# Four accumulator banks for the first layer, and one small exponential of ScalarE in the value stage

## The chip, the cores and the metric

The kernel runs on one core of a Trainium2 chip. The metric is the device time of one execution in microseconds (us). The core has TensorE (matmuls; its results go to PSUM, which has 8 banks of 2 KB in each of 128 partitions), VectorE, ScalarE, GpSimd and SyncE, which here issues most transfers. The engines run by their own lists of instructions and meet only at semaphores.

## The reference

One layer of attention over a graph of 384 nodes with 1024 features and 16 heads of 64, with a residual and a layer norm:

```python
q = x @ wq.T + bq
k = x @ wk.T + bk
v = x @ wv.T + bv
q2 = (q @ wiq.T + biq).reshape(N, H, D).transpose(1, 0, 2)
k2 = (k @ wik.T + bik).reshape(N, H, D).transpose(1, 0, 2)
v2 = (v @ wiv.T + biv).reshape(N, H, D).transpose(1, 0, 2)
mask = _build_mask(edge_index, edge_type, edge_type_weights, x.dtype)
scores = jnp.einsum('hnd,hmd->hnm', q2, k2) * scale + mask[None]
attn = jax.nn.softmax(scores, axis=-1)
out = jnp.einsum('hnm,hmd->hnd', attn, v2)
out = out.transpose(1, 0, 2).reshape(N, OUT_F)
return out @ wo.T + bo
```

The result is `_layernorm(x + that)`. The mask (384 x 384) is filled from 6144 edges; of several edges for one cell the last one counts.

## The kernel before

**Arithmetic.** Every float32 factor is split in two: a high part in a reduced format (`w_hi`, `h_hi`), and a low part, the rest (`w_lo`, `h_lo`). A product is three matmuls: high by high, high by low, low by high (lines 888 to 890). The high part is made by ScalarE (line 393 for weights, 440 for the first layer's results), and the low part by VectorE (600, 682) or GpSimd (307) as raw minus high.

**Stages.** Weights come as 56 tiles of 128 x 1024 through a ring of RING = 4 slots. Tiles 0 to 23 are the first layer (q, k and v, eight each): each is 24 matmuls into one bank. The loop over groups (`group`, Fori from 1 to 5) handles four tiles a turn; group 0 stands ahead of it, and its tiles 0 and 1 are done together. Tiles 24 to 31 are the value stage (v2 of all nodes, in banks 0 to 5). Tiles 32 to 47 are q and k of the eight head pairs. A step of the attention handles the q and k tile of pair j on TensorE, and woven in between scores, transposes and values of pair a = j - 1. Tiles 48 to 55 are the output product, woven into the last pair.

**Order in the first layer.** For tile t TensorE waits for `w_lo` of t (`tile_ready`) and, in the loop, for `acc_free` of at least t + 1; the semaphore starts at 2, so this says that tile t - 2 has been emptied. `first_acc` (banks 4 and 5) serves tiles 0 and 1, `acc` (banks 6 and 7) all later ones by turns. A finished tile is read by ScalarE (line 440, h_hi), then by VectorE (line 682, h_lo), and this second read frees the bank. VectorE's order is: w_lo of tiles 2 to 5 with the emptying of tiles 0 to 3 between, the table of edge values (`value_table`), then eight counts of edges for group 0 (line 664, `count_later`), and then the loop. A turn of the loop is, four times over: w_lo of tile t + 2 (600), one count, emptying of tile t (682), one count. In its first turn, t is 4, so w_lo of tile 6 stands ahead of the emptying of tile 4.

**Order in the value stage and the attention.** In the value stage ScalarE makes w_hi of tile t + 2 once tile t - 2 is through (`split`). In the step of the first pair it takes the biased results of the k tile (456), two w_hi, a copy of the values (480, `v_high`), then the exponentials of five of the six score tiles (486). VectorE masks the scores (773, negated row maximum beside it), and normalises with the reciprocal of the row sums (781, 783). TensorE transposes the probs of one head once all its three tiles are normalised (977, waits `probs_ready`). VectorE's first mask waits also for `mask_loaded` and for `res_ready`, three additions of GpSimd (358) that come after its 48 scatters of mask cells (336) and three w_lo.

**Function tables of ScalarE.** Exp, Ln and Sqrt want a table loaded; the build puts a table load (ACT_TABLE_LOAD) ahead of the activation that needs another table than the one that is there. Before, there are four: at lines 388, 428 (Ln), 486 (Exp) and 568 (Sqrt). Copy and Identity run with any of these.

Of the kernel before, what the change touches and what calls it, by code (L numbers as in the profile page):

```python
# [11 lines left out]
ACT = mybir.ActivationFunctionType  # L12
ALU = mybir.AluOpType
AX_X = mybir.AxisListType.X
ds = bass.ds

P = 128
N = 384
# [20 lines left out]
RING = 4  # L39
L1_TILES = 3 * KT  # L40
IV_TILE = L1_TILES
# [9 lines left out]
FIRST_TILES = 2  # L51
# [11 lines left out]
def gnn_layer(nc, x_t, x_rows, weights, bias_cols, bias_rows, edge_weights, edge_cols, edge_rows,  # L63
              key_rows, mask_cells, out):
    with ExitStack() as ctx:
        def sb(name, shape, dt):
            return ctx.enter_context(nc.sbuf_tensor(name, shape, dt))

        def sem(name):
            return ctx.enter_context(nc.semaphore(name))  # L70
# [3 lines left out]
        x_hi, x_lo = sb("x_hi", [P, KT, N], F32R), sb("x_lo", [P, KT, N], F32R)  # L74
        att_hi, att_lo = x_hi, x_lo

        h_hi, h_lo = sb("h_hi", [P, L1_TILES, N], F32R), sb("h_lo", [P, L1_TILES, N], F32R)
# [39 lines left out]
        def x_raw(k):  # L117
# [15 lines left out]
        ew, ew_abs, ew_exp, ew_ln, ew_pos, soft = (  # L133
            sb(n, [P, ETYPES], F32) for n in ("ew", "ew_abs", "ew_exp", "ew_ln", "ew_pos", "soft"))
        zeros = sb("zeros", [P, P], F32)
# [6 lines left out]

        bank = [ctx.enter_context(nc.psum_tensor(f"bank{i}", [P, HALF], F32)) for i in range(8)]
        acc = bank[6:8]
        first_acc = bank[4:6]
        score_bank = [bank[i] for i in (0, 1, 2, 3, 0, 1)]

        def pt_bank(a, g):
# [34 lines left out]
        acc_free = sem("acc_free")  # L183
# [197 lines left out]
        def _(act):  # L381
# [8 lines left out]
            def high_part(t, s, raws):  # L390

                act.wait_ge(raw_loaded[s], 16 * raws)
                nc.scalar.activation(w_part(t, s, slice(0, F))[0], w_raw[:, s, :], ACT.Copy).then_inc(w_hi_done, 1)  # L393

            def split(t, s, raws):

                act.wait_ge(tile_done, t - RING + 1)
                high_part(t, s, raws)
# [31 lines left out]
            def group(g, first=False):  # L430
                for s in range(RING):
                    t = RING * g + s


                    if not (first and s == 0):
                        high_part(t + LEAD, (s + LEAD) % RING, g + 1 + (s + LEAD) // RING)

                    act.wait_ge(tile_done, t + 1)
                    ps = first_acc[s] if first and s < FIRST_TILES else acc[s % 2]
                    nc.scalar.activation(h_hi[:, ds(t, 1), :].rearrange("p a n -> p (a n)"), ps[:, 0:N],  # L440
                                         ACT.Identity, bias=bcol[:, ds(t, 1)]).then_inc(acc_hi, 1)

            group(0, first=True)
            with act.Fori(1, GROUPS) as g:
                group(g)


            for t in range(IV_TILE, PAIR_TILE):
                split(t + LEAD, (t + LEAD) % RING, (t + LEAD) // RING + 1)

            def evacuate(t, u, slot, which):

                act.wait_ge(tile_done, t + 1)
                for h in range(2):
                    here = slice(h * D, (h + 1) * D)
                    nc.scalar.activation((q_high, k_parts)[which][here, 2 * slot + h, :], acc[which][here, 0:N],
                                         ACT.Identity, bias=bcol[here, ds(u, 1)]).then_inc(half_hi, 1)
# [85 lines left out]
            a = PAIRS - 1  # L543
# [34 lines left out]
        def _(dve):  # L578
# [16 lines left out]
            def low_part(t, s):  # L595

                dve.wait_ge(w_hi_done, t + 1)
                cols = slice(0, F)
                hi, lo = w_part(t, s, cols)
                nc.vector.tensor_tensor(lo, w_raw[:, s, cols], hi.bitcast(F32), ALU.subtract)\  # L600
                    .then_inc(w_lo_dve, 1)
# [59 lines left out]
            def count_later(g, slot, chunks):  # L661
                for c in chunks:
                    n = P * (WC - c % WC)
                    nc.vector.scalar_tensor_tensor(  # L664
                        out=unread[:, c, 0:n],
                        in0=keyb[:, slot, P * c:P * c + n].rearrange("p a e -> p (a e)"),
                        scalar=key[:, ds(GC * g + c, 1)], in1=later[:, 0:n],
                        op0=ALU.is_equal, op1=ALU.mult, accum_out=n_later[:, ds(GC * g + c, 1)]).then_inc(dve_step, 1)
                    steps[1] += 1

            def choose_cells(g):
                mine = ds(GC * g, GC)

                dve.wait_ge(dve_step, steps[0] + steps[1])
                nc.vector.scalar_tensor_tensor(out=cell[:, mine], in0=n_later[:, mine], scalar=BEYOND,
                                               in1=key[:, mine], op0=ALU.mult, op1=ALU.add)\
                    .then_inc(cells_ready, 1)

            def evacuate(t, ps):

                dve.wait_ge(acc_hi, t + 1)
                nc.vector.scalar_tensor_tensor(  # L682
                    out=h_lo[:, ds(t, 1), :].rearrange("p a n -> p (a n)"), in0=ps[:, 0:N],
                    scalar=bcol[:, ds(t, 1)],
                    in1=h_hi[:, ds(t, 1), :].rearrange("p a n -> p (a n)").bitcast(F32),
                    op0=ALU.add, op1=ALU.subtract).then_inc(acc_free, 1)
# [3 lines left out]
            def group(g, slot):  # L690
                t = RING * g
                for s in range(RING):
                    low_part(t + LEAD + s, (LEAD + s) % RING)
                    if s == 0:

                        dve.wait_ge(rows_loaded, 16 * g + 16)
                    count_later(g, slot, range(2 * s, 2 * s + 1))
                    evacuate(t + s, acc[s % 2])
                    count_later(g, slot, range(2 * s + 1, 2 * s + 2))
                choose_cells(g)  # L700

            for t in range(FIRST_TILES):
                low_part(t + LEAD, t + LEAD)
                evacuate(t, first_acc[t])
            low_part(FIRST_TILES + LEAD, 0)
            evacuate(FIRST_TILES, acc[0])
            value_table()
            low_part(FIRST_TILES + 1 + LEAD, 1)
            evacuate(FIRST_TILES + 1, acc[1])

            dve.wait_ge(rows_loaded, 16)
            count_later(0, ds(0, 1), range(GC))
# [3 lines left out]
            with dve.Fori(1, GROUPS) as g:  # L716
                new_part(STEPS_PER_GROUP * g + (before - STEPS_PER_GROUP))
                group(g, ds(g % 2, 1))
                assert steps[1] == STEPS_PER_GROUP
# [128 lines left out]
            a = PAIRS - 1  # L848
# [7 lines left out]
            for n in range(NT):  # L856
                for i, (b, cols) in enumerate(OUT_PIECES[n]):
# [4 lines left out]
                    ins = nc.vector.bn_stats(stats[:, n, 6 * i:6 * i + 6], part)  # L862
# [14 lines left out]
        def _(pe):  # L877
            def tile_ready(t, pair_tile=False):

                if pair_tile:  # L880
                    pe.wait_ge(w_lo_pool, t + 1 - PAIR_TILE)
                else:
                    pe.wait_ge(w_lo_dve, t + 1)

            def by_outputs(out_ps, s, k, moving_hi, moving_lo):

                cols = slice(k * P, (k + 1) * P)
                pe.matmul(out_ps, w_hi[:, s, cols], moving_hi, start=(k == 0), stop=False)  # L888
                pe.matmul(out_ps, w_hi[:, s, cols], moving_lo, start=False, stop=False)  # L889
                return pe.matmul(out_ps, w_lo[:, s, cols], moving_hi, start=False, stop=(k == KT - 1))  # L890
# [17 lines left out]
            for k in range(KT):  # L908
                pe.wait_ge(x_lo_done, k + 1)
                for t in range(FIRST_TILES):  # L910
                    if k == 0:
                        pe.wait_ge(first_half_lo, t + 1)
                    if k == KT // 2:
                        tile_ready(t)
                    ins = by_outputs(first_acc[t][:, 0:N], t, k, x_hi[:, k, :], x_lo[:, k, :])
                    if k == KT - 1:
                        ins.then_inc(tile_done, 1)

            def group(g, slots=range(RING)):
                for s in slots:  # L920
                    t = RING * g + s
                    tile_ready(t)

                    if not isinstance(g, int):
                        pe.wait_ge(acc_free, t + 1)
                    for k in range(KT):
                        ins = by_outputs(acc[s % 2][:, 0:N], s, k, x_hi[:, k, :], x_lo[:, k, :])
                    ins.then_inc(tile_done, 1)

            group(0, range(FIRST_TILES, RING))  # L930
            with pe.Fori(1, GROUPS) as g:
                group(g)


            for k in range(KT):
                t = IV_TILE + k
# [121 lines left out]
            a = PAIRS - 1  # L1058
# [98 lines left out]
```

## Time and profile before

| | us |
|---|---|
| median of 3 runs | 299.97 |
| the runs | 299.97, 1647.63, 299.97 |
| the profiled execution | 299.66 |
| its span, from the first to the last instruction | 297.9 |
| TensorE busy | 289.7 |
| VectorE busy | 200.7 |
| ScalarE busy | 175.8 |
| GpSimd busy | 142.5 |

The mean granted TensorE clock was 0.997 of full speed. Busy times are sums over the span; matmuls overlap in the pipeline, so the rows of two matmuls that follow each other start closer together than each is long. The time from one start to the next is the one that counts.

### The profile page before, as it was taken

Reading aid. Unit: us, or ns where it says so; the run is one execution under the profiler, and the core shown is the slowest. Engines: PE = TensorE matmul, PEld = TensorE weight load, DVE = VectorE, ACT = ScalarE, POOL = GpSimd, SP = SyncE. Lnnn points to the kernel's source line nnn. Section 1 sums busy time; section 2 is a strip of 40 time slices with the busy share of each in tenths; the row PEclk is TensorE's granted clock in tenths of the full one; section 3 lists DMA queues with packets and bytes.
Section 4 is the critical chain, followed back from the end, with each engine's and each line's share of the span. In section 5 each row is a group of like instructions: output and inputs, shape, how many; then the busy total and the mean of one; then the engine's idle time right before and its main releaser. Section 6 shows DMA issues by size and latency. Waiting matters only on the chain.

```text
span 297.9 us, 5259 instructions
## 1 busy us (share of the span) xinstructions
PE 289.7 (97%) x1640; PEld 274.0 (92%) x1640; DVE 200.7 (67%) x494; ACT 175.8 (59%) x330; POOL 142.5 (48%) x124
## 2 busy tenths in 40 slices
PE   8999899999999999999998999999999999999992
PEld 8999899999999998888998999999999998887882
DVE  4869967677666764204458798888888888843184
ACT  5863244323443352221299899999999999934432
POOL 2000635535556452659953445545463637845600
PEclk9999999999999999999999999999999999999998
DMA  7978556363662448826210404030312121410013
GB/s 219 379 251 310 178 177 211 108 181 135 207 217 79 134 141 320 315 73 185 105 41 31 142 0 143 12 130 25 116 47 94 59 82 70 150 64 0 2 70 141
DMA packets 14318, 39.83 MB, mean 134 GB/s; under 512 B 3200, under 2 KB 4832, under 8 KB 14176
## 3 DMA queue, kind: packets, MB, share of 16 engines
q1 hardware_dynamic: 12192, 38.38, 37.7%
q0 software_dynamic: 1680, 0.62, 1.1%
q10 hardware_dynamic: 432, 0.66, 0.8%
q8 instruction: 7, 0.11, 0.2%
q14 instruction: 7, 0.06, 0.1%
HBM read 37.44 MB, written 2.21 MB: 133 GB/s over the span
## 4 chain that ended last, share of the span: by engine, by line
PE 89%; DVE 5%; ACT 4%; issue 1%; DVEq 0%; ACTq 0%
PE bank L897 21%; PE bank L888 17%; PE bank L890 17%; PE bank L889 17%; PE bank L994 6%; PE bank L977 5%; PE bank L963 2%; PE bank L967 2%; PE bank L906 2%; DVE res L664 1%; ACT probs L486 1%; ACT w_hi L393 1%; ACT L486 0%; DVE w_lo L600 0%; DVE h_lo L790 0%
## 5 line engine op out<-in xcount | busy, mean ns | idle before, releaser
L336 POOL DMA_INDIRECT mask_cells<-cell_value,cell x48 | 54.9, 1143 | 75.0 <-DMA mask_cells<-cell_value,cell 31.0
L307 POOL TENSOR_TENSOR w_lo<-w_raw,w_hi 128x1024 fp32r<-128x1024 f32 x20 | 47.6, 2403 | 44.1 <-DVE probs L783 40.2
L888 PE MATMUL bank<-x_hi,w_hi 128*128 128x384 f32 x192 | 64.4, 336 | 0.8 <-DVE h_lo L682 0.8
L393 ACT ACTIVATE w_hi<-w_raw 128x1024 fp32r<-128x1024 f32 x50 | 52.4, 1054 | 20.8 <-PE bank L897 19.6
L889 PE MATMUL bank<-x_lo,w_hi 128*128 128x384 f32 x192 | 64.2, 334 | 0.0
L890 PE MATMUL bank<-x_hi,w_lo 128*128 128x384 f32 x192 | 64.2, 334 | 0.0
L440 ACT ACTIVATE h_hi<-bank,bcol 128x384 f32 (+1 forms) x24 | 14.0, 582 | 58.1 <-PE bank L890 58.1
L888 PE MATMUL bank<-h_hi,w_hi 128*128 128x384 f32 x128 | 46.4, 362 | 0.0
L600 DVE TENSOR_TENSOR w_lo<-w_raw,w_hi 128x1024 fp32r<-128x1024 f32 x30 | 36.6, 1222 | 12.5 <-ACT w_hi L393 10.1
L890 PE MATMUL bank<-h_hi,w_lo 128*128 128x384 f32 x128 | 43.0, 336 | 0.0
L889 PE MATMUL bank<-h_lo,w_hi 128*128 128x384 f32 x128 | 42.9, 335 | 0.0
L888 PEld LDWEIGHTS bank<-x_hi,w_hi 128*128 128x128 f32 x192 | 36.0, 188 | 1.4 <-issue 1.1
L889 PEld LDWEIGHTS bank<-x_lo,w_hi 128*128 128x128 f32 x192 | 36.0, 188 | 0.0
L890 PEld LDWEIGHTS bank<-x_hi,w_lo 128*128 128x128 f32 x192 | 36.0, 188 | 0.0
L790 DVE TENSOR_TENSOR h_lo<-bank,h_hi 128x384 fp32r<-128x384 f32 x48 | 26.0, 555 | 10.8 <-ACT h_hi L496 10.3
L773 DVE CUSTOM_DVE_ANT_0 probs<-bank,mask 128x384 f32<-128x384 f32 x48 | 25.4, 555 | 9.3 <-PE bank L967 9.1
L486 ACT ACTIVATE probs<-probs,neg_max 128x384 f32<-128x384 f32 x48 | 29.2, 609 | 3.7 <-DVE neg_max L773 3.6
L682 DVE SCALAR_TENSOR_TENSOR h_lo<-bank,bcol,h_hi 128x384 f32 (+1 forms) x24 | 14.8, 617 | 24.2 <-ACT h_hi L440 24.2
L496 ACT ACTIVATE h_hi<-bank 128x384 fp32r<-128x384 f32 x48 | 22.3, 485 | 8.2 <-PE bank L977 7.5
L664 DVE SCALAR_TENSOR_TENSOR res<-probs,key,res 128x512 uint8<-128x512 bf16 (+7 forms) x48 | 25.6, 545 | 0.0
L977 PE MATMUL bank<-ident,probs 128*128 128x128 f32 x144 | 23.6, 272 | 0.8 <-DVE probs L783 0.8
L889 PEld LDWEIGHTS bank<-h_lo,w_hi 128*128 128x128 f32 x128 | 24.2, 189 | 0.0
(103 smaller groups left out, 530.2 us busy)
## 6 DMA issues: line engine op xcount, KB each, us to landing
w_raw<-weights SPq DMA_DIRECT2D x54, 512.0 KB, 3.3
probs<-key_rows SPq DMA_DIRECT2D x6, 512.0 KB, 3.8
res<-x_rows SPq DMA_DIRECT2D x1, 1536.0 KB, 6.8
out<-res SPq DMA_DIRECT2D x6, 256.0 KB, 2.0
v<-x_t SPq DMA_DIRECT2D x6, 192.0 KB, 5.7
w_raw<-weights SPq DMA_DIRECT2D x3, 256.0 KB, 5.8
mask_cells<-cell_value,cell POOLq DMA_INDIRECT x48
mask_cells<-mask SPq DMA_DIRECT2D x1, 576.0 KB, 4.1
```

What stands on the lines that cost most here:

```text
L307: nc.gpsimd.tensor_tensor(lo, w_raw[:, s, cols], hi.bitcast(F32), ALU.subtract)\
L336: nc.gpsimd.indirect_dma_start(out=mask_cells, out_offset=bass.IndirectOffsetOnAxis(ap=cell[:, c:c + 1], axis=0), in_=cell_value[:, c:c + ...
L393: nc.scalar.activation(w_part(t, s, slice(0, F))[0], w_raw[:, s, :], ACT.Copy).then_inc(w_hi_done, 1)
L486: nc.scalar.activation(probs[:, i, :], probs[:, i, :], ACT.Exp, bias=neg_max[:, i:i + 1], scale=-1.0, accum_out=row_sum[:, i:i + 1]).then_ ...
L600: nc.vector.tensor_tensor(lo, w_raw[:, s, cols], hi.bitcast(F32), ALU.subtract)\
L664: nc.vector.scalar_tensor_tensor(out=unread[:, c, 0:n], in0=keyb[:, slot, P * c:P * c + n].rearrange("p a e -> p (a e)"), scalar=key[:, ds ...
L790: nc.vector.tensor_tensor(pt_lo[:, g % 3, :], pt_bank(a, g)[:, 0:N], pt_hi[:, g % 3, :].bitcast(F32), ALU.subtract)\
L888: pe.matmul(out_ps, w_hi[:, s, cols], moving_hi, start=(k == 0), stop=False)
L889: pe.matmul(out_ps, w_hi[:, s, cols], moving_lo, start=False, stop=False)
L890: return pe.matmul(out_ps, w_lo[:, s, cols], moving_hi, start=False, stop=(k == KT - 1))
L897: ins = pe.matmul(bank[b][:, 0:cols.stop - cols.start], left, w_part(t, t % RING, cols)[which], start=(start and i == 0), stop=(stop and i ...
L977: ins = pe.transpose(pt_bank(a, g)[:, b * P:(b + 1) * P], probs[:, 2 * b + h, m * P:(m + 1) * P], ident[:, :])
```

## The change

The first layer takes a bank by slot: tiles use banks 4, 5, 6, 7 in turn (`layer_acc`), for TensorE's matmuls, ScalarE's read and VectorE's read alike. TensorE's wait in the loop goes from t + 1 to t - RING + 3, which is t - 1: tile t - 4 has been emptied. The pair tiles of the attention stay on banks 6 and 7. In the value stage ScalarE runs a one-column exponential of zeros behind w_hi of tile 30; its result is not used.

```diff
-        first_acc = bank[4:6]
+        layer_acc = bank[4:8]
...
                     act.wait_ge(tile_done, t + 1)
-                    ps = first_acc[s] if first and s < FIRST_TILES else acc[s % 2]
-                    nc.scalar.activation(h_hi[:, ds(t, 1), :].rearrange("p a n -> p (a n)"), ps[:, 0:N],
+                    nc.scalar.activation(h_hi[:, ds(t, 1), :].rearrange("p a n -> p (a n)"), layer_acc[s][:, 0:N],
                                          ACT.Identity, bias=bcol[:, ds(t, 1)]).then_inc(acc_hi, 1)
...
             for t in range(IV_TILE, PAIR_TILE):
                 split(t + LEAD, (t + LEAD) % RING, (t + LEAD) // RING + 1)
+                if t == IV_TILE + RING:
+
+                    nc.scalar.activation(ew_abs[:, 0:1], zeros[:, 0:1], ACT.Exp)
...
-            def evacuate(t, ps):
+            def evacuate(t, s):
...
-                    out=h_lo[:, ds(t, 1), :].rearrange("p a n -> p (a n)"), in0=ps[:, 0:N],
+                    out=h_lo[:, ds(t, 1), :].rearrange("p a n -> p (a n)"), in0=layer_acc[s][:, 0:N],
...
-                    evacuate(t + s, acc[s % 2])
+                    evacuate(t + s, s)
...
-                    ins = by_outputs(first_acc[t][:, 0:N], t, k, x_hi[:, k, :], x_lo[:, k, :])
+                    ins = by_outputs(layer_acc[t][:, 0:N], t, k, x_hi[:, k, :], x_lo[:, k, :])
...
                     if not isinstance(g, int):
-                        pe.wait_ge(acc_free, t + 1)
+
+                        pe.wait_ge(acc_free, t - RING + 3)
                     for k in range(KT):
-                        ins = by_outputs(acc[s % 2][:, 0:N], s, k, x_hi[:, k, :], x_lo[:, k, :])
+                        ins = by_outputs(layer_acc[s][:, 0:N], s, k, x_hi[:, k, :], x_lo[:, k, :])
```

**TensorE, head of the loop over the first layer's groups.** Before, the first matmul of a turn carried both waits:

```order
L890 MATMUL bank<-x_hi,w_lo 128x384
L931 UNCONDITIONAL_BRANCH
L931 ISA
L888 MATMUL bank<-x_hi,w_hi 128x384 [waits acc_free,w_lo_dve]
L889 MATMUL bank<-x_lo,w_hi 128x384
L890 MATMUL bank<-x_hi,w_lo 128x384
```

Of the change, the same place:

```order
L893 MATMUL bank<-x_hi,w_lo 128x384
L935 UNCONDITIONAL_BRANCH
L935 ISA
L929 REGISTER_ALU [waits w_lo_dve]
L891 MATMUL bank<-x_hi,w_hi 128x384 [waits acc_free]
L892 MATMUL bank<-x_lo,w_hi 128x384
L893 MATMUL bank<-x_hi,w_lo 128x384
```

The two thresholds now differ, so a register instruction works out the second one, and the wait for w_lo sits on it. The other three tiles of a turn keep both waits on their first matmul.

**ScalarE, value stage, from w_hi of tile 28 on.** Before:

```order
L393 ACTIVATE w_hi<-w_raw 128x1024 [waits raw_loaded0,tile_done]
L393 ACTIVATE w_hi<-w_raw 128x1024 [waits raw_loaded1,tile_done]
L393 ACTIVATE w_hi<-w_raw 128x1024 [waits raw_loaded2,tile_done]
L393 ACTIVATE w_hi<-w_raw 128x1024 [waits raw_loaded3,tile_done]
L393 ACTIVATE w_hi<-w_raw 128x1024 [waits raw_loaded0,tile_done]
```

Of the change:

```order
L394 ACTIVATE w_hi<-w_raw 128x1024 [waits raw_loaded0,tile_done]
L394 ACTIVATE w_hi<-w_raw 128x1024 [waits raw_loaded1,tile_done]
L394 ACTIVATE w_hi<-w_raw 128x1024 [waits raw_loaded2,tile_done]
L452 ACT_TABLE_LOAD
L452 ACTIVATE ew_abs<-zeros 128x1
L394 ACTIVATE w_hi<-w_raw 128x1024 [waits raw_loaded3,tile_done]
```

A table load and the small exponential stand between w_hi of tile 30 and of tile 31.

**ScalarE, step of the first head pair, ahead of the exponentials.** Before:

```order
L393 ACTIVATE w_hi<-w_raw 128x1024 [waits raw_loaded3,tile_done]
L393 ACTIVATE w_hi<-w_raw 128x1024 [waits raw_loaded0,tile_done]
L480 ACTIVATE vp<-v 128x6x64 [waits v2_ready]
L486 ACT_TABLE_LOAD
L486 ACTIVATE probs,row_sum<-probs,neg_max 128x384 [waits masked] x5
```

Of the change:

```order
L394 ACTIVATE w_hi<-w_raw 128x1024 [waits raw_loaded3,tile_done]
L394 ACTIVATE w_hi<-w_raw 128x1024 [waits raw_loaded0,tile_done]
L483 ACTIVATE vp<-v 128x6x64 [waits v2_ready]
L489 ACTIVATE probs,row_sum<-probs,neg_max 128x384 [waits masked] x5
L394 ACTIVATE w_hi<-w_raw 128x1024 [waits raw_loaded1,tile_done]
```

The table load here is gone; the count of table loads in the program is four before and after.

## Rows read from the trace of the kernel before

**Rows 1.** The page: busy time (part 1), and the chain that ended last.
```profile
PE 289.7 (97%) x1640; PEld 274.0 (92%) x1640; DVE 200.7 (67%) x494; ACT 175.8 (59%) x330; POOL 142.5 (48%) x124
...
PE 89%; DVE 5%; ACT 4%; issue 1%; DVEq 0%; ACTq 0%
```

**Rows 2.** Waits of TensorE: who for whom, us in total, times, longest.
```profile
PE bank L977 <- DVE probs L783: 0.8, 1, 0.8
PE bank L888 <- DVE h_lo L682: 0.8, 1, 0.8
```

**Rows 3.** Timeline: start, us, engine, line, operation [idle before]; matmuls, a weight load.
```profile
32.07 0.34 PE L890 MATMUL bank<-x_hi,w_lo 128*128 128x384 f32 x1
33.21 0.41 PE L888 MATMUL bank<-x_hi,w_hi 128*128 128x384 f32 x1 [0.81 <-DVE h_lo L682]
...
31.90 0.19 PEld L890 LDWEIGHTS bank<-x_hi,w_lo 128*128 128x128 f32 x1
```

**Rows 4.** Timeline of VectorE around tile 6.
```profile
30.64 1.22 DVE L600 TENSOR_TENSOR w_lo<-w_raw,w_hi 128x1024 fp32r<-128x1024 f32 x1 [0.48 <-issue]
...
32.46 0.61 DVE L682 SCALAR_TENSOR_TENSOR h_lo<-bank,bcol,h_hi 128x384 f32 x1
```

**Rows 5.** Timeline of ScalarE: reads of finished tiles 5, 6, 7.
```profile
32.57 0.58 ACT L440 ACTIVATE h_hi<-bank,bcol 128x384 f32 x1 [2.63 <-PE bank L890]
...
37.80 0.58 ACT L440 ACTIVATE h_hi<-bank,bcol 128x384 f32 x1 [3.70 <-PE bank L890]
...
41.96 0.58 ACT L440 ACTIVATE h_hi<-bank,bcol 128x384 f32 x1 [2.63 <-PE bank L890]
```

**Rows 6.** Timeline of TensorE, first and second attention steps, and the start of the third.
```profile
151.34 0.62 PE L963 MATMUL bank<-h_lo,h_hi 128*128 128x384 f32 x2
...
152.14 0.34 PE L888 MATMUL bank<-h_hi,w_hi 128*128 128x384 f32 x1
...
158.18 0.55 PE L977 MATMUL bank<-ident,probs 128*128 128x128 f32 x3 [0.82 <-DVE probs L783]
...
167.06 0.51 PE L963 MATMUL bank<-h_lo,h_hi 128*128 128x384 f32 x2
...
167.75 0.33 PE L888 MATMUL bank<-h_hi,w_hi 128*128 128x384 f32 x1
...
172.78 0.52 PE L977 MATMUL bank<-ident,probs 128*128 128x128 f32 x3
...
181.63 0.51 PE L963 MATMUL bank<-h_lo,h_hi 128*128 128x384 f32 x2
```

**Rows 7.** Timeline of ScalarE ahead of the first exponentials.
```profile
152.55 0.51 ACT L480 ACTIVATE vp<-v 128x384 fp32r<-128x384 f32 x1
153.07 1.28 ACT L486 ACT_TABLE_LOAD   x1
154.37 0.62 ACT L486 ACTIVATE probs<-probs,neg_max 128x384 f32<-128x384 f32 x1
```

**Rows 8.** Timeline of VectorE in the first attention step.
```profile
152.43 0.56 DVE L773 CUSTOM_DVE_ANT_0 probs<-bank,mask 128x384 f32<-128x384 f32 x1 [1.15 <-PE bank L967]
...
154.77 0.56 DVE L773 CUSTOM_DVE_ANT_0 probs<-bank,mask 128x384 f32<-128x384 f32 x1 [0.17 <-PE bank L967]
...
157.51 0.16 DVE L781 RECIPROCAL row_inv<-row_sum 128x1 f32<-128x1 f32 x1 [0.25 <-ACT probs L486]
157.71 0.42 DVE L783 TENSOR_SCALAR probs<-probs,row_inv 128x384 f32<-128x384 f32 x1
```

**Rows 9.** Timeline of ScalarE in the value stage, tiles 30 and 31.
```profile
120.68 1.06 ACT L393 ACTIVATE w_hi<-w_raw 128x1024 fp32r<-128x1024 f32 x1 [3.02 <-PE bank L897]
124.76 1.06 ACT L393 ACTIVATE w_hi<-w_raw 128x1024 fp32r<-128x1024 f32 x1 [3.02 <-PE bank L897]
```

**Rows 10.** Group of GpSimd's scatters (busy, mean ns, idle before), its additions in the timeline.
```profile
L336 POOL DMA_INDIRECT mask_cells<-cell_value,cell x48 | 54.9, 1143 | 75.0 <-DMA mask_cells<-cell_value,cell 31.0
...
141.66 7.11 POOL L358 TENSOR_TENSOR res<-res,probs 128x1024 f32<-128x1024 f32 x3
```

More of the change, by code:

```diff
@@ L703, in _ @@
                 low_part(t + LEAD, t + LEAD)
-                evacuate(t, first_acc[t])
+                evacuate(t, t)
             low_part(FIRST_TILES + LEAD, 0)
-            evacuate(FIRST_TILES, acc[0])
+            evacuate(FIRST_TILES, FIRST_TILES)
             value_table()
             low_part(FIRST_TILES + 1 + LEAD, 1)
-            evacuate(FIRST_TILES + 1, acc[1])
+            evacuate(FIRST_TILES + 1, FIRST_TILES + 1)
             dve.wait_ge(rows_loaded, 16)
```

## The prediction

> **What bounds the kernel now.** I first read the busy shares and the chain that ended last [rows 1]: TensorE is busy 289.7 us of a span of 297.9 us, and the chain runs through it for 89% of the span. So only time in which TensorE stands still, at places where it isn't standing still for its own sake, can be won. The view of waits of TensorE shows how little there is [rows 2]: one wait of 0.8 us for VectorE's h_lo (line 682), one of 0.8 us for VectorE's probs (line 783). The rest of the 8.2 us is the start and the tail after the last matmul, which the change doesn't touch. Each of the two edits is aimed at one of these waits, so the question is what each wait costs with its surroundings, and what is late next.
>
> **First stall: tile 6 of the first layer.** Tiles 0 to 23 follow each other on TensorE, 24 matmuls each, and a layer tile t may not start before its bank has been emptied by VectorE. Before, tiles from 2 on alternate between two banks, so tile 6 waits for the emptying of tile 4. The timeline shows a matmul starting at 32.07, the next one only at 33.21 [rows 3], right behind VectorE's h_lo that started at 32.46 and took 0.61, to 33.07 [rows 4]. VectorE is late there since it counts edges for group 0 before it enters the loop. The price is read from ScalarE's reads of finished tiles: tile 5 at 32.57, tile 6 at 37.80, tile 7 at 41.96 [rows 5]. A tile without a wait takes 41.96 - 37.80 = 4.16 us; tile 6 took 5.23. So the stall costs **1.07 us**, the idle 0.81 and a restart of the matmul pipeline.
>
> **What the four banks do to it.** With bank s for slot s, tile t needs only tile t-4 emptied; tile 6 needs tile 2. Tile 2 ended three tiles before tile 5, some 12.5 us (3 x 4.16), and is long emptied. What is late next is w_lo of tile 6, the other thing that tile 6 waits for: VectorE makes it from 30.64 to 31.86 [rows 4]. Without a wait the weight load of tile 6 would follow the last one of tile 5, at 31.90, by the usual 0.17, at 32.07 [rows 3]; from the end of VectorE's h_lo (33.07) to the matmul it released (33.21) it is 0.14. Ready at 31.86 + 0.14 = 32.00 against 32.07: hidden by 0.07 us only. Bounds for what remains: nothing below, and above, if the release is slower, some 0.3 us. I take 0. Tile 7's w_lo follows the emptying at 32.46 by about 0.6 for it, 0.7 for a count and 1.2 for itself, so it is ready near 35.0 (an estimate from [rows 4]); TensorE will want it one tile after 32.2, at 36.4. Later tiles showed no wait in a loop of the same order [rows 2]. The extra register instruction at the loop's head, which now carries the wait on w_lo by itself, exists in the same form in the loop over head pairs, where TensorE shows no wait at its head [rows 2]: I take 0, and put its upper bound for the 5 passes at 0.3 too. Banks 4 and 5 are used next by the value stage, whose first matmul waits already for the emptying of tile 22, so nothing new is waited for. Gain: 1.07 us.
>
> **Second stall: the first transposes of the attention.** In the step of the first head pair TensorE must wait for the normalised probs of one head, which need five exponentials of ScalarE. ScalarE ends the copy of the values (152.55 + 0.51 = 153.06), then runs a table load of 1.28 us from 153.07, and the first exponential only at 154.37 [rows 7]. Its input had been ready since 152.43 + 0.56 = 152.99 [rows 8]. VectorE's last piece starts at 157.71 and takes 0.42, and the transposes start at 158.18 [rows 6, 8]. The price comes from comparing this step with the next, which does the same work: from the first score matmul to the first transpose it is 158.18 - 151.34 = 6.84 us, and 172.78 - 167.06 = 5.72 us one step later: 1.12 more. Of this 0.11 lies in the scores before (152.14 - 151.34 = 0.80 against 167.75 - 167.06 = 0.69), which the change doesn't touch. That leaves 1.01. Over the whole step it is 167.06 - 151.34 = 15.72 against 181.63 - 167.06 = 14.57, or 1.15; less the same 0.11, **1.04 us**. I take this [rows 6].
>
> **What moving the table load does.** The small exponential makes the load run in the value stage, between w_hi of tiles 30 and 31. There ScalarE works from 120.68 for 1.06 and then waits for TensorE until 124.76 [rows 9]: 3.02 us idle. The load (1.28) and a one-column exponential (below the 0.62 of a 384-wide one [rows 7]) take at most 1.9 of it and cost nothing; if that cover were gone, w_hi of tile 31 would come late by as much, and TensorE needs it only after tiles 28 to 30, 12 us later. Copies and biased reads behind it need no other table: the program has still four table loads. In the attention the chain becomes 153.08 for the first exponential instead of 154.37, 1.29 earlier. The masked scores come at 152.99 and then up to the fifth at 154.77 + 0.56 = 155.33 [rows 8]; one exponential takes (157.51 - 154.37) / 5 = 0.63, the fifth would start at 153.08 + 4 x 0.63 = 155.6, so it still isn't held by them. VectorE's last reciprocal moves from 157.51 to 156.22, the probs end at 156.84, and transposes could start at 156.9. TensorE itself wants to start them at 158.18 - 1.01 = 157.17. Covered by about 0.3 us, so the whole 1.04 is won, and the rest of the 1.29 is slack. Bounds: 1.04 at best, and if masks or reciprocals bind by up to 0.3 us, 0.75.
>
> The Trainium skill (ScalarE: Activation LUTs, What ACT_TABLE_LOAD costs) gives a switch of tables a second part, a drain of about 1.38 us beside the 1.28 of the load, some 2.66 in all. This trace doesn't agree at this place: between the copy's end and the first exponential lie 1.31 us, all of it the load. By that figure the sum would stay the same, since TensorE's own pace caps it, but the load's own 1.38 more would leave no cover to speak of in the value stage (3.02 - 2.66 = 0.36, less the small exponential).
>
> **The sum.** 1.07 + 1.04 = 2.11 us. Both stalls delay all that TensorE does behind them, and from there to the end it shows no idle until its last matmul, so the gains add up and reach the end. The span goes from 297.9 to 295.8 us and the profiled execution's 299.66 to 297.55. The median of the three runs is 299.97, 0.31 above the profiled one; by it the time would be 297.86. I forecast **297.8 us**.
>
> **The rivals.**
> *A. The forecast, both stalls gone:* 297.4 to 298.3. Chance 0.72.
>
> *B. One stall lives on in another wait.* For the first, w_lo of tile 6 has a cover of only 0.07 us [rows 3, 4]; for the second, the masks and the reciprocals have 0.3. If a residue of 0.3 to 1 us stays, the time is 298.3 to 299.2. For it speaks how thin the covers are; against it that each can be late only by the engine's own small variations, since VectorE's chain up to 31.86 doesn't change. Chance 0.17.
>
> *C. The change doesn't do what it says:* the table load or the bank wasn't what TensorE stood for, and another semaphore of the same instruction comes at the same moment. Then 299.5 to 300.2. Against it: the table load stands in the gap with no idle on either side [rows 7], and VectorE's h_lo ends 0.14 before the matmul. Chance 0.05.
>
> *D. Slower, by GpSimd's scatter.* GpSimd's 48 scatters of mask cells take 54.9 us and their waits 75 [rows 10]; behind them come its w_lo tiles and the three additions to res, which end at 141.66 + 7.11 = 148.77 [rows 10]. VectorE may not mask the first scores before that. Now it starts at 152.43; with the first gain it would start at 151.36, so the chain may be 2.6 us later before it costs anything. Beyond that each microsecond is one of TensorE's at the first transposes. It eats up the whole gain at 2.6 + 2.1 = 4.7 us, and is 2% slower (306) only at 2.6 + 8.2 = 10.8 us. The scatters could be stretched, since they take 1.14 us in the mean and VectorE's work beside them now lies 1 us differently. The mean of all 48 would have to grow by 0.1 for 4.7 us. Against it: the waits between them are DMA's and not VectorE's for the most part, and the work beside them is the same in kind. A typical case would give 300 to 303. Chance 0.04. The Trainium skill (SBUF — State Buffer, Who interferes with whom) says that a VectorE instruction with two SBUF inputs contends with a GpSimd instruction that reads SBUF; by that rule a shift of VectorE's work against the scatters could stretch or shorten them either way, and no row here splits that off.
>
> *E. More than forecast*, 296.5 to 297.4, if the restarts cost more than the two comparisons show. Chance 0.02.
>
> **How the numbers follow.** A, E and most of B make up the range: 297.0 to 299.2 us, with 0.9 of the chance by the cases and some less by my doubt in them. About 2% (6 us) is what a measurement can tell from no change, and no case but the far end of D leaves it: within 2% 0.97, slower 0.02, faster 0.01.
>
> **What would show each step.** The waits of TensorE should have neither row of [rows 2]. Reads of finished tiles by ScalarE should be 4.16 us apart from tile 5 to 6 too; if they are 4.2 to 4.5 apart, w_lo of tile 6 is the residue. A table load of 1.28 us should stand alone in the value stage with over 1 us idle behind it, the first exponential should follow the copy of the values at once, and first score to first transpose should be about 5.8 us. GpSimd's additions to res should still end near 149 us, more than 2 us before the first mask. The forecast is wrong if a wait of over 0.3 us shows at either place, or if TensorE gets a wait somewhere in steps that had none.

## The result

The changed kernel takes 297.61 us (median of 6 runs, 297.33 to 297.82) where the kernel before takes 299.95 us. The ratio is 0.9924, with a 95% interval of 0.9914 to 0.9935, or 2.0 to 2.6 us. The forecast was 297.8 us, within 2% of before. The profiled execution took 297.57 us (forecast 297.55), its span is 295.8 us (forecast 295.8). One run of 1647.63 us of the kernel before and one of 305.86 us of the kernel with GpSimd late (below) were far slower than the rest; they enter no ratio, and move their kernel's median by under 0.05 us.

The page of the changed kernel, its busy times and its last chain, against [rows 1]:

```profile
PE 289.2 (98%) x1640; PEld 274.3 (93%) x1640; DVE 200.8 (68%) x494; ACT 175.9 (59%) x331; POOL 141.3 (48%) x124
...
PE 96%; DVE 1%; ACT 1%; issue 0%
```

TensorE is busy for as long as before (within 0.5 us), in a span that is 2.1 us shorter. The chain that ended last ran through VectorE and ScalarE for 9%, and now does for 2%. Before, it left TensorE for two long detours, from 19.96 to 33.21 us and from 149.54 to 158.18 us, each of which ends at one of the two stalls; both are gone. The shares are the length of the detours and not what they cost. In the waits of TensorE both rows of [rows 2] are gone, and only the wait at the start is left, which was there before too:

```profile
PE bank L909 <- DVE zeros L593: 1.1, 1, 1.1
```

**First layer.** ScalarE's reads of tiles 5, 6 and 7, against [rows 5], are now evenly spaced, 4.15 us and 4.16 us:

```profile
32.56 0.58 ACT L440 ACTIVATE h_hi<-bank,bcol 128x384 f32 x1 [2.63 <-PE bank L893]
...
36.71 0.58 ACT L440 ACTIVATE h_hi<-bank,bcol 128x384 f32 x1 [2.62 <-PE bank L893]
...
40.87 0.58 ACT L440 ACTIVATE h_hi<-bank,bcol 128x384 f32 x1 [2.63 <-PE bank L893]
```

VectorE hasn't changed, against [rows 4]. The emptying of tile 4 ends as late as before, at 33.06, but nobody waits for it:

```profile
30.63 1.22 DVE L603 TENSOR_TENSOR w_lo<-w_raw,w_hi 128x1024 fp32r<-128x1024 f32 x1 [0.47 <-issue]
...
32.45 0.61 DVE L685 SCALAR_TENSOR_TENSOR h_lo<-bank,bcol,h_hi 128x384 f32 x1
```

The weight loads of TensorE at the same place, the last one of tile 5 and the first one of tile 6, against [rows 3], follow each other by 0.17. The wait on w_lo of tile 6 sits ahead of the second one, and w_lo ended at 30.63 + 1.22 = 31.85, 0.2 us before it:

```profile
31.89 0.19 PEld L893 LDWEIGHTS bank<-x_hi,w_lo 128*128 128x128 f32 x1
32.06 0.19 PEld L891 LDWEIGHTS bank<-x_hi,w_hi 128*128 128x128 f32 x1
```

**Value stage.** ScalarE around the moved table load, against [rows 9]. The load starts 0.02 after the end of w_hi of tile 30, the small exponential 0.01 after the load, and behind it 1.50 us of idle time are left before w_hi of tile 31:

```profile
119.59 1.06 ACT L394 ACTIVATE w_hi<-w_raw 128x1024 fp32r<-128x1024 f32 x1 [3.02 <-issue]
120.67 1.28 ACT L452 ACT_TABLE_LOAD   x1
121.96 0.20 ACT L452 ACTIVATE ew_abs<-zeros 128x1 f32<-128x1 f32 x1
123.67 1.06 ACT L394 ACTIVATE w_hi<-w_raw 128x1024 fp32r<-128x1024 f32 x1 [1.50 <-PE bank L900]
```

**First attention step.** ScalarE's copy of the values is followed at once by the first exponential, against [rows 7]:

```profile
151.46 0.51 ACT L483 ACTIVATE vp<-v 128x384 fp32r<-128x384 f32 x1
151.94 0.62 ACT L489 ACTIVATE probs<-probs,neg_max 128x384 f32<-128x384 f32 x1
```

VectorE's first and fifth mask and last piece of probs in that step, against [rows 8]:

```profile
151.34 0.56 DVE L776 CUSTOM_DVE_ANT_0 probs<-bank,mask 128x384 f32<-128x384 f32 x1 [1.15 <-PE bank L971]
...
153.66 0.56 DVE L776 CUSTOM_DVE_ANT_0 probs<-bank,mask 128x384 f32<-128x384 f32 x1 [0.17 <-PE bank L971]
...
155.28 0.42 DVE L786 TENSOR_SCALAR probs<-probs,row_inv 128x384 f32<-128x384 f32 x1
```

TensorE's first score matmul, first transpose, and the first score matmuls of the next two steps, against [rows 6]:

```profile
150.25 0.61 PE L967 MATMUL bank<-h_lo,h_hi 128*128 128x384 f32 x2
...
156.08 0.49 PE L981 MATMUL bank<-ident,probs 128*128 128x128 f32 x3
...
164.92 0.51 PE L967 MATMUL bank<-h_lo,h_hi 128*128 128x384 f32 x2
...
179.48 0.51 PE L967 MATMUL bank<-h_lo,h_hi 128*128 128x384 f32 x2
```

From first score to first transpose it is 5.83 us (before 6.84, one step later 5.72), and the whole step takes 164.92 - 150.25 = 14.67 us instead of 15.72: 1.05 us. The next step takes 14.56.

**GpSimd.** Its additions to res, against [rows 10], end at 140.53 + 7.10 = 147.63, 1.1 us earlier than before:

```profile
140.53 7.10 POOL L359 TENSOR_TENSOR res<-res,probs 128x1024 f32<-128x1024 f32 x3
```

### The profile page after: what moved, and what is told of

It reads as the page before. It is cut to its first block, busy times and chain, and to the rows that moved or that the text cites. A ratio compares the mean times of both kernels' runs of the same rounds, so it can differ in the third digit from the quotient of the medians.

```text
span 295.8 us, 5260 instructions
## 1 busy us (share of the span) xinstructions
PE 289.2 (98%) x1640; PEld 274.3 (93%) x1640; DVE 200.8 (68%) x494; ACT 175.9 (59%) x331; POOL 141.3 (48%) x124
## 4 chain that ended last, share of the span: by engine, by line
PE 96%; DVE 1%; ACT 1%; issue 0%
PE bank L900 21%; PE bank L891 19%; PE bank L893 19%; PE bank L892 19%; PE bank L998 6%; PE bank L981 5%; PE bank L967 3%; PE bank L971 3%; PE bank L909 2%; DVE h_lo L793 0%; ACT h_hi L499 0%; ACT res L576 0%; ACT h_hi L394 0%; DVE att_sum L767 0%; DVE stats L865 0%
## 5 line engine op out<-in xcount | busy, mean ns | idle before, releaser
L337 POOL DMA_INDIRECT mask_cells<-cell_value,cell x48 | 53.6, 1117 | 75.1 <-DMA mask_cells<-cell_value,cell 31.3
L891 PEld LDWEIGHTS bank<-h_hi,w_hi 128*128 128x128 f32 x128 | 24.1, 188 | 0.0
```

The costliest lines, as they stand in the source:

```text
L337: nc.gpsimd.indirect_dma_start(out=mask_cells, out_offset=bass.IndirectOffsetOnAxis(ap=cell[:, c:c + 1], axis=0), in_=cell_value[:, c:c + ...
```

## The experiments

The profiled executions don't start equally fast: the read of tile 5 by ScalarE stands between 32.35 and 33.02 us in the nine traces of this study, though the edits hardly touch what comes ahead of it (another bank in some kernels, one small fill of VectorE in one). Part of that shows as waits of TensorE in the first 8 us, ahead of every edit: 0.24 and 0.33 us in the kernel with late exponentials, 0.23 in the one with GpSimd late. So the last two columns take that read as zero and give what is left of the span behind it. They are 0.1 us sharp, since the page gives the span in tenths. Each ratio is to runs of the kernel before made beside that kernel; their medians were 299.69 to 299.95 us.

| kernel | median us | ratio to before, 95% interval | span | read of tile 5 | span behind it | against before |
|---|---|---|---|---|---|---|
| before | 299.95 | | 297.9 | 32.57 | 265.3 | |
| the change | 297.61 | 0.9924 (0.9914 to 0.9935) | 295.8 | 32.56 | 263.2 | -2.1 |
| banks only | 298.87 | 0.9970 (0.9959 to 0.9981) | 296.6 | 32.35 | 264.3 | -1.1 |
| small exponential only | 298.62 | 0.9965 (0.9951 to 0.9978) | 296.9 | 32.48 | 264.4 | -0.9 |
| two banks, half the counts | 298.57 | 0.9968 (0.9957 to 0.9980) | 296.8 | 32.47 | 264.3 | -1.0 |
| change, w_lo late | 297.85 | 0.9931 (0.9914 to 0.9947) | 296.4 | 33.02 | 263.4 | -1.9 |
| change, exponentials late | 298.30 | 0.9945 (0.9929 to 0.9962) | 296.5 | 32.70 | 263.8 | -1.5 |
| change, GpSimd late | 298.97 | 0.9968 (0.9956 to 0.9980) | 297.1 | 32.83 | 264.3 | -1.1 |
| change, w_lo later | 300.14 | 1.0024 (1.0010 to 1.0038) | 298.3 | 32.94 | 265.4 | 0.0 |

### Each half alone

The four banks without the small exponential:

```diff
-                if t == IV_TILE + RING:
-
-                    nc.scalar.activation(ew_abs[:, 0:1], zeros[:, 0:1], ACT.Exp)
```

> The four banks alone, without the small exponential. Theory (two separate stalls, 1.07 us and 1.04 us, that add up): span 297.9 - 1.07 = 296.8 us, some 1.07 us under the kernel before and 1.04 over the changed one; ScalarE's reads of tiles 5, 6, 7 are 4.16 us apart; the wait of 0.8 us for VectorE's probs stays, with first score to first transpose 6.84 us. Rival (the gains hide each other, since the second stall's ScalarE chain starts from TensorE): the span differs from 296.8 by over 0.3 us. On GpSimd's scatters: if they run by their own waits for DMA, the additions to res still end at 148.8 us; if they follow VectorE's counts, which follow TensorE, they end about 1.1 us earlier, near 147.7.

The small exponential in the kernel before:

```diff
             for t in range(IV_TILE, PAIR_TILE):
                 split(t + LEAD, (t + LEAD) % RING, (t + LEAD) // RING + 1)
+                if t == IV_TILE + RING:
+
+                    nc.scalar.activation(ew_abs[:, 0:1], zeros[:, 0:1], ACT.Exp)
```

> The small exponential alone, with the two alternating banks. Theory: span 297.9 - 1.04 = 296.9 us; the wait of 0.8 us for VectorE's h_lo at tile 6 stays, tile 6 is read 5.23 us after tile 5; first score to first transpose falls from 6.84 to about 5.8 us; a table load of 1.28 us stands alone in the value stage behind w_hi of tile 30. Rival (ScalarE's table was not what TensorE waited for): the 6.84 us stay and the span is 297.9 us. GpSimd's additions to res end at 148.8 us in any case, as the first layer isn't moved.

Each removes one wait and leaves the other. Of the banks alone, the wait of TensorE that is left, ScalarE's reads of tiles 5 and 6, TensorE's first score and first transpose, and GpSimd's additions to res, in this order:

```profile
PE bank L978 <- DVE probs L783: 0.8, 1, 0.8
```

```profile
32.35 0.58 ACT L440 ACTIVATE h_hi<-bank,bcol 128x384 f32 x1 [2.63 <-PE bank L890]
...
36.51 0.58 ACT L440 ACTIVATE h_hi<-bank,bcol 128x384 f32 x1 [2.62 <-PE bank L890]
```

```profile
150.05 0.62 PE L964 MATMUL bank<-h_lo,h_hi 128*128 128x384 f32 x2
...
156.89 0.55 PE L978 MATMUL bank<-ident,probs 128*128 128x128 f32 x3 [0.85 <-DVE probs L783]
```

```profile
140.51 7.12 POOL L359 TENSOR_TENSOR res<-res,probs 128x1024 f32<-128x1024 f32 x3
```

Tile 6 is read 4.16 us after tile 5, and first score to first transpose is 6.84 us, as before. Of the exponential alone, the wait that is left, TensorE's three matmuls, and GpSimd's additions:

```profile
PE bank L891 <- DVE h_lo L685: 0.8, 1, 0.8
```

```profile
151.25 0.62 PE L966 MATMUL bank<-h_lo,h_hi 128*128 128x384 f32 x2
...
157.11 0.49 PE L980 MATMUL bank<-ident,probs 128*128 128x128 f32 x3
...
165.93 0.51 PE L966 MATMUL bank<-h_lo,h_hi 128*128 128x384 f32 x2
```

```profile
141.49 7.15 POOL L358 TENSOR_TENSOR res<-res,probs 128x1024 f32<-128x1024 f32 x3
```

First score to first transpose is 5.86 us here, the step 14.68. Behind the read of tile 5 the two halves give 1.1 and 0.9 us, together 2.0 against 2.1 for the change: they add up, and neither hides the other. The ratios say the same within their intervals (0.9 and 1.0 us, against 2.3).

GpSimd's additions end at 147.63 with the banks and at 148.64 without. So the scatters, which come ahead of these additions, move with the first layer. This part of the expectation had two sides, and the second one held.

### Too few banks, or VectorE late?

The kernel before, with two banks, and only half of group 0's counts. The edges that are not counted get a count of 1, which marks them as overwritten by a later edge, so this kernel leaves them out of the mask:

```diff
-            count_later(0, ds(0, 1), range(GC))
+            count_later(0, ds(0, 1), range(GC // 2))
...
             nc.vector.memset(mask[:, :, :], NEG)
+            nc.vector.memset(n_later[:, :], 1.0)
```

> The kernel before with its two alternating banks, but VectorE counts only the first four of group 0's eight chunks ahead of the loop; the other four chunks' edges are left out of the mask (512 of 6144). Theory (tile 6 waits because VectorE is late from its counts, not because two banks are too few as such): VectorE comes some 1.9 us earlier to the emptying of tile 4, the wait of TensorE at tile 6 is gone with two banks too, tile 6 is read 4.16 us after tile 5 and the span is 296.8 us. Rival (two banks can't run without a wait when the loop is entered): a wait of 0.3 to 0.8 us stays there and the span is over 297.2 us.

VectorE's w_lo of tile 6 and the emptying of tile 4, and ScalarE's reads of tiles 5 and 6:

```profile
28.23 1.22 DVE L601 TENSOR_TENSOR w_lo<-w_raw,w_hi 128x1024 fp32r<-128x1024 f32 x1
...
30.04 0.61 DVE L683 SCALAR_TENSOR_TENSOR h_lo<-bank,bcol,h_hi 128x384 f32 x1
```

```profile
32.47 0.58 ACT L440 ACTIVATE h_hi<-bank,bcol 128x384 f32 x1 [2.63 <-PE bank L891]
...
36.62 0.58 ACT L440 ACTIVATE h_hi<-bank,bcol 128x384 f32 x1 [2.62 <-PE bank L891]
```

The emptying of tile 4 ends at 30.65 instead of 33.07, 2.4 us earlier, more than the 1.9 us of the four counts, since the idle time of 0.48 at the loop's entry is missing too. The reads are 4.15 us apart with two banks, and the span behind tile 5 is 1.0 us shorter. So the stall was VectorE's lateness behind its counts; the two more banks are a buffer for it. As the steady state of the loop shows, two banks would do where VectorE is on time.

In this trace the first scatter starts at 29.17 us instead of 31.15, and GpSimd's additions to res end at 146.44 us, 1.2 us earlier than in the changed kernel, whose first layer runs at the same pace. So the scatters don't follow the first layer alone. Their own start counts too, or the fewer cells that they store here; this run doesn't part the two.

### How close is w_lo of tile 6?

The changed kernel with two fills on VectorE ahead of the loop:

```diff
             choose_cells(0)
+            for spare in (att_half, att_sum):
+                nc.vector.memset(spare, 0.0)
             before = steps[1]
```

> The changed kernel with two fills of 128x384 on VectorE (some 0.4 to 0.5 us each) between group 0's counts and the loop, so that w_lo of tile 6 comes later. In the changed kernel it ends at 31.85 us, and TensorE would load its weights at 32.06 us. Theory (the next wait of tile 6 is w_lo, with a cover of 0.1 us): TensorE stands still at tile 6, and the read of tile 6 comes 4.16 us plus the delay less 0.1 us after that of tile 5: 4.9 us if the fills delay by their full 0.9 us, 4.4 if part of them hides in the loop's entry; the span grows by the same 0.3 to 0.8 us. Rival (w_lo of tile 6 has a cover of a microsecond or more): 4.16 us stay and the span is 295.8 us.

The two fills and w_lo of tile 6, then ScalarE's reads of tiles 5 and 6:

```profile
30.64 0.38 DVE L718 MEMSET att_half<- 128x384 f32 x1
31.05 0.38 DVE L718 MEMSET att_sum<- 128x384 f32 x1
31.35 1.16 DVE L603 TENSOR_TENSOR w_lo<-w_raw,w_hi 128x1024 fp32r<-128x1024 f32 x1
```

```profile
33.02 0.58 ACT L440 ACTIVATE h_hi<-bank,bcol 128x384 f32 x1 [2.64 <-PE bank L895]
...
37.20 0.58 ACT L440 ACTIVATE h_hi<-bank,bcol 128x384 f32 x1 [2.65 <-PE bank L895]
```

The reads are 4.18 us apart, not 4.4 to 4.9. The delay that was meant didn't come about: w_lo ended at 32.51, which is 0.51 before the read of tile 5, where in the changed kernel it is 32.56 - 31.85 = 0.71. The 0.8 us of fills cost only 0.2; the idle time of 0.47 that the changed kernel has ahead of the loop's first instruction is missing. Even so the trace shows how thin the cover is. These are TensorE's last weight load of tile 5 and its first one of tile 6:

```profile
32.34 0.19 PEld L895 LDWEIGHTS bank<-x_hi,w_lo 128*128 128x128 f32 x1
32.56 0.19 PEld L893 LDWEIGHTS bank<-x_hi,w_hi 128*128 128x128 f32 x1
```

They are 0.22 us apart instead of 0.17, and the second starts 0.05 after the end of w_lo: a delay of 0.2 us has just used the cover up. To see what a delay beyond it costs, the next kernel has two fills of 128x1024 more:

```diff
-            for spare in (att_half, att_sum):
+            for spare in (att_half, att_sum, v2[:, 0, :], v2[:, 1, :]):
```

> As e4_w_lo_late, where two fills moved w_lo of tile 6 by only 0.2 us since the rest hid in the loop's entry, with two more fills of 128x1024 (0.9 us each, an estimate from the 1.02 us of the 128x1152 fill of the mask). Theory (cover of w_lo of tile 6 is 0.1 to 0.2 us): w_lo of tile 6 comes 2.0 us later against tile 5 than in the changed kernel, and the read of tile 6 comes 1.8 to 1.9 us later, 6.0 us after that of tile 5; TensorE shows a wait for w_lo. Rival (cover of over a microsecond, the small effect of e4 being no sign of it): the read of tile 6 comes under 1 us later.

The wait of TensorE, VectorE's w_lo of tile 6, ScalarE's reads of tiles 5 and 6:

```profile
PE bank L893 <- DVE w_lo L603: 1.9, 1, 1.9
```

```profile
33.42 1.16 DVE L603 TENSOR_TENSOR w_lo<-w_raw,w_hi 128x1024 fp32r<-128x1024 f32 x1
```

```profile
32.94 0.58 ACT L440 ACTIVATE h_hi<-bank,bcol 128x384 f32 x1 [2.64 <-PE bank L895]
...
39.25 0.58 ACT L440 ACTIVATE h_hi<-bank,bcol 128x384 f32 x1 [4.79 <-PE bank L895]
```

Now w_lo ends at 34.58, 1.64 after the read of tile 5: 2.35 later than in the changed kernel. The reads are 6.31 us apart, a stall of 2.15. The cover is the difference, **0.2 us**. What lies beyond it is paid in full: from the kernel with two fills to this one w_lo comes 2.15 us later and the read of tile 6 2.13. The gain is given back. In the trace the span behind tile 5 is that of the kernel before; by the runs the kernel is 0.24% slower (0.10 to 0.38%), but its ten runs fall in two groups, six of 299.8 to 300.2 us, to which the profiled one belongs, and four of 301.1 to 301.4 us, and no trace shows why. The expected 1.8 to 1.9 us were short by the longer delay (2.35 instead of 2.0).

### How close is the chain of the exponentials?

```diff
                     v_high(a, 1 - par)
+                    if isinstance(j, int) and a == 0:
+                        for spare in (att_half, att_sum):
+                            nc.scalar.activation(spare, v2[:, 0, 0:N], ACT.Copy)
```

> The changed kernel with two copies of 128x384 on ScalarE (0.51 us each in the trace, about 1.0 us together) between the copy of the values and the first exponential of the first step. Theory (the exponentials' chain has a cover of 0.2 us there: probs end at 155.70 us, transposes' weight load at 155.91 us): transposes start about 0.8 us later, first score to first transpose is 6.6 us instead of 5.83, and the span is 296.6 us. Rival (the masks of VectorE bind, so that ScalarE has slack of its own): under 0.4 us of delay.

ScalarE's copy of the values, the two extra copies and the first exponential; TensorE's first score and first transpose:

```profile
151.60 0.51 ACT L483 ACTIVATE vp<-v 128x384 fp32r<-128x384 f32 x1
152.01 0.51 ACT L517 ACTIVATE att_half<-v 128x384 f32<-128x384 f32 x1
152.43 0.51 ACT L517 ACTIVATE att_sum<-v 128x384 f32<-128x384 f32 x1
152.84 0.60 ACT L489 ACTIVATE probs<-probs,neg_max 128x384 f32<-128x384 f32 x1
```

```profile
150.39 0.61 PE L970 MATMUL bank<-h_lo,h_hi 128*128 128x384 f32 x2
...
156.64 0.55 PE L984 MATMUL bank<-ident,probs 128*128 128x128 f32 x3 [0.24 <-DVE probs L789]
```

Measured from the first score, the first exponential comes 2.45 us later instead of 1.69: the two copies delay it by 0.76, since copies that follow each other overlap (0.41 from start to start, not 0.51). First score to first transpose goes from 5.83 to 6.25 us, 0.42. So the cover was 0.76 - 0.42 = 0.34 us. The expected 0.8 us of delay counted the copies at 0.51 and the cover at 0.2. It lies just over the 0.4 us under which the rival theory would have stood. That VectorE's last reciprocal waits for ScalarE again decides for ScalarE:

```profile
155.97 0.16 DVE L787 RECIPROCAL row_inv<-row_sum 128x1 f32<-128x1 f32 x1 [0.25 <-ACT probs L489]
```

### How close is GpSimd?

```diff
+                    spare = probs[:, :, :].rearrange("p a b -> p (a b)")[:, F:2 * F]
+                    for i in range(2):
+                        nc.gpsimd.tensor_tensor(spare, res[:, 0, :], bo_row, ALU.add).then_inc(pool_step, 1)
+                        pool.wait_ge(pool_step, 3 + i)
                     for n in range(NT):
                         nc.gpsimd.tensor_tensor(res[:, n, :], res[:, n, :], bo_row, ALU.add).then_inc(res_ready, 1)
```

> The changed kernel with two more additions of 128x1024 on GpSimd (2.37 us each, 4.74 together) ahead of the three additions to res. In the changed kernel these end at 147.63 us and VectorE's first mask starts at 151.34 us. Theory (the cover of GpSimd's chain is 3.7 us): the additions end at 152.4 us, the first mask starts 1.0 to 1.1 us later, w_lo of tile 35 ends near 154.8 us and TensorE is held up by 0.8 to 1.2 us in all; span 296.6 to 297.0 us. Rival (the cover is larger, or the delay is taken up by slack further on): under 0.4 us.

GpSimd's three additions, VectorE's first mask and the wait of TensorE:

```profile
145.70 7.11 POOL L363 TENSOR_TENSOR res<-res,probs 128x1024 f32<-128x1024 f32 x3
```

```profile
152.99 0.56 DVE L780 CUSTOM_DVE_ANT_0 probs<-bank,mask 128x384 f32<-128x384 f32 x1 [2.52 <-POOL res L363]
```

```profile
154.09 0.61 PE L971 MATMUL bank<-h_lo,h_hi 128*128 128x384 f32 x2 [0.85 <-DVE neg_max L780]
```

The additions end at 152.81 and hold up the first mask, which starts 152.99 - 150.52 = 2.47 us after the first score instead of 1.09: 1.38 later. The step takes 1.1 us longer, and the span behind tile 5 is 1.0 us longer, as expected. But TensorE stands at the third pair of score matmuls, which wait for two masked tiles, and not at the transposes or at w_lo of tile 35. In the changed kernel the first mask starts 3.71 us after the additions (147.63 to 151.34), and here 0.18 us after them (152.81 to 152.99), so the cover of GpSimd's chain was 3.5 us. Against the read of tile 5 the additions end 4.91 us later than in the changed kernel, and 4.91 - 1.38 gives the same. The expectation had taken all of the 3.7.

## Why the prediction was right, point by point

- **First stall, 1.07 us.** Right in size and in cause. Reads of 5.23 us became 4.15 us (1.08). The banks alone gave 1.1 us, and half the counts with two banks 1.0 us, so what had been late was VectorE. What the prediction calls a restart beside the idle 0.81 is mostly overlap: the row of the matmul ahead of the idle time is 0.34 us long, where its follower usually starts after 0.17. From start to start it was 33.21 - 32.07 = 1.14 instead of 0.17, which is 0.97 of the 1.07; the matmuls behind it, first 0.25 apart instead of 0.17, give the rest.
- **What is late next at tile 6.** w_lo, as said. The cover was put at 0.07 us and is 0.2 us: the release was taken at 0.14, from a matmul that waited for VectorE's h_lo, where the weight load of tile 6 starts 0.05 after the end of w_lo in both kernels with fills. The step's sign held with little room: by these figures (an estimate, no run has this delay) 0.5 us more on VectorE would have left 0.3 us, the lower end of rival B.
- **The extra register instruction.** Nothing, as taken: TensorE shows no wait at any turn of the loop.
- **Second stall, 1.04 us.** The step became 1.05 us shorter. Comparing it with the same work one step later gave the price better than the idle row, which says 0.8.
- **The cap by TensorE's own pace.** The exponentials came 1.3 us earlier and 1.04 were won. The cover was put at about 0.3 us and measured at 0.34.
- **The place of the moved table load.** 1.50 us idle left behind it. The estimate of the small exponential as below 0.62 was wide; it took 0.20.
- **The drain of the Trainium skill** (ScalarE: Activation LUTs, What ACT_TABLE_LOAD costs). The trace of the changed kernel disagrees here as well: 0.02 us ahead of the load and 0.01 behind it, at the new place too.
- **The sum.** 2.11 forecast, 2.1 in the trace, 2.0 to 2.6 by the interval of the runs.
- **Rival D's numbers.** Wrong in one step: "with the first gain it would start at 151.36, so the chain may be 2.6 us later". It took GpSimd's scatters to stand still while TensorE moves. They moved along by 1.1 us, the additions still ended 3.7 us ahead of the first mask, and the chain could be 3.5 us later before the mask was. And TensorE would have been held at the scores, not at the transposes. Neither touched the forecast, but both mean that the rival was priced from a wrong place.

Why the scatters move along stays open. GpSimd's longest wait for them (5.93 us) lies beside the load of res and of weight tiles, whose start follows the first layer, but that can't be where the shift comes from: ahead of it the scatters are already 1.05 us earlier (98.78 us in the change against 99.83 before). No run takes the loads of weights away or shifts them alone.

## What to carry to other kernels

When one engine is busy for 97% of the span, list its waits one by one, and price each by comparing its stretch with the same work elsewhere, not by the idle time alone (1.07 for an idle row of 0.81, 1.04 for one of 0.82). Then look for the next signal at the same instruction: here the gain at tile 6 stood on 0.2 us of cover, and 2.35 us of delay on VectorE cost as much as the whole change had won. More buffers paid here only because the engine that empties them was late for a while; and the table load cost nothing where its engine waited anyway.

## What the runs showed of the hardware

- The load of Exp's table on ScalarE took 1.28 us in all nine traces, in two different places of the program, with 0.01 to 0.02 us ahead of it and behind it. In the path it cost 1.34 us: from the start of the copy of the values to that of the first exponential it is 154.37 - 152.55 = 1.82 us with the load between them and 151.94 - 151.46 = 0.48 without.
- Small work ahead of VectorE's loop was nearly free in one kernel: 0.8 us of fills moved the end of the loop's first instruction by only 0.2 us against TensorE, since 0.47 us of idle time at the loop's entry was missing. It was missing as well in the kernel with half the counts, which has no fills there. So it isn't simply hidden beside them, and its cause stays open; the place of the code is one candidate, and no run tests it.
- ScalarE copies of 128x384 that follow each other start 0.41 us apart, though each is 0.51 us long.
- The read of tile 5 stands anywhere from 32.35 to 33.02 us in nine traces, though the edits hardly touch what comes ahead of it. Spans of single executions that differ by under 0.7 us should be compared from a common event on.
